# Splitting into high and low parts, moved: spread over attention slots, rounded on ScalarE in the feed-forward, half of the next norm taken forward

## The reference

```python
qkv = hidden_states @ w_qkv.T                 # 1: attention, 16 heads of 16
q, k, v = jnp.split(qkv, 3, axis=-1)
q = _rms_norm(q, q_norm_w); k = _rms_norm(k, k_norm_w)
q = _rope(q); k = _rope(k)                    # per head
scores = jnp.where(mask, q @ k^T * scale, -inf)   # causal, window of 128
out = softmax(scores) @ v
x = x + out @ w_o.T

y1 = x1 @ w_up + b_up + x1 @ w_up_lora_a @ w_up_lora_b    # 2: 256 -> 1024
x2 = relu(y1)
y2 = x2 @ w_down + b_down + x2 @ w_down_lora_a @ w_down_lora_b

proj = x @ W_xproj.T + b_xproj                # 3: selective scan
dt = softplus(dt_r @ W_dt.T + b_dt)
h = scan(exp(dt * A), dt * Bm * x);  y = sum_n h * Cm
```

## Time and profile before

| | us |
|---|---|
| median of three runs (lowest, highest) | 1144.26 (1142.16, 1153.11) |
| the profiled execution, its own time | 1144.68 |
| its span on the core | 1142.5 |

### The profile page before, as it was taken

The page is one execution under the profiler, slowest core; times in us unless marked ns, Lnnn a source line. Parts: engine busy times, 40 slices in busy tenths (PEclk is TensorE's granted clock), DMA queues, the critical chain, the costliest instruction groups (busy, mean ns, idle before and its releaser), DMA issues. The chain is left out here.

```text
span 1142.5 us, 21388 instructions
## 1 busy us (share of the span) xinstructions
PE 1038.2 (91%) x6931; PEld 908.6 (80%) x6931; DVE 800.7 (70%) x1860; ACT 689.4 (60%) x1963; POOL 650.6 (57%) x688
## 2 busy tenths in 40 slices
PE   3798987896899769999999999999979999999998
PEld 2687876685455368999999999999968888888887
DVE  6676765726888857888888888888875555555555
ACT  3455544326799758887878788877844343343432
POOL 5334312541777568786877687766634555555453
PEclk9789989898899889999999999999989999999999
DMA  9000000001224002110011000000011111111111
GB/s 254 2 1 1 2 18 5 13 1 56 95 88 144 13 1 84 47 36 3 2 47 38 1 2 2 1 2 2 1 44 30 54 41 51 45 41 55 41 46 46
DMA packets 44082, 41.58 MB, mean 36 GB/s; under 512 B 6160, under 2 KB 40048, under 8 KB 44000
## 3 DMA queue, kind: packets, MB, share of 16 engines
q1 hardware_dynamic: 42384, 39.54, 11.5%
q10 hardware_dynamic: 1616, 0.99, 0.3%
HBM read 39.40 MB, written 1.11 MB: 35 GB/s over the span
## 5 line engine op out<-in xcount | busy, mean ns | idle before, releaser
L1829 POOL TENSOR_TENSOR prob<-prob,rden 128x128 f32<-128x128 f32 (+1 forms) x256 | 127.9, 521 | 83.0 <-DVE rden L1910 81.0
L2198 POOL TENSOR_TENSOR hid_l<-hid,hid_h 128x512 fp32r<-128x512 f32 x66 | 85.4, 1294 | 133.6 <-ACT hid_h L2167 133.6
L2225 DVE TENSOR_TENSOR hid<-psum,silu 128x512 f32<-128x512 f32 x66 | 45.6, 692 | 124.7 <-ACT silu L2165 124.7
L2165 ACT ACTIVATE silu<-psum 128x512 f32<-128x512 f32 x66 | 39.5, 598 | 115.3 <-PE psum L75 115.3
L2217 DVE SCALAR_TENSOR_TENSOR x<-psum,weight,x 128x256 f32<-128x256 f32 x264 | 108.9, 476 | 0.0
L73 PE MATMUL psum<-xt_h,gu_l 128*128 128x512 f32 x264 | 106.0, 402 | 0.3 <-DVE xt_l L167 0.3
L1775 ACT ACTIVATE prob<-psum,neg_max 128x128 f32<-128x128 f32 (+1 forms) x256 | 104.9, 420 | 0.2
L75 PE MATMUL psum<-xt_h,gu_h 128*128 128x512 f32 x264 | 104.8, 397 | 0.0
L74 PE MATMUL psum<-xt_l,gu_h 128*128 128x512 f32 x264 | 104.5, 396 | 0.0
L1300 POOL TENSOR_TENSOR drive<-u,b_all 128x1024 f32<-128x1024 f32 x32 | 75.6, 2365 | 41.9 <-DVE h L1416 20.6
L1812 POOL TENSOR_TENSOR qr<-r_part_a,r_part_b 128x512 f32<-128x512 f32 x64 | 82.7, 1292 | 6.5 <-DVE r_part_b L1867 6.5
(11 more groups left out here) (281 smaller groups left out, 3748.2 us busy)
## 6 DMA issues: line engine op xcount, KB each, us to landing
b_all<-scan_b_rows SPq DMA_DIRECT2D x16, 512.0 KB, 3.9
early<-in_L_ffn_Wq_dram SPq DMA_DIRECT2D x4, 1024.0 KB, 5.8
early<-in_L_ffn_Wo_dram SPq DMA_DIRECT2D x4, 1024.0 KB, 6.0
raw<-in_L_ffn_Wg_dram SPq DMA_DIRECT2D x32, 128.0 KB, 2.2
raw<-in_L_ffn_Wu_dram SPq DMA_DIRECT2D x32, 128.0 KB, 2.3
raw<-in_L_ffn_Wd_dram SPq DMA_DIRECT2D x32, 128.0 KB, 2.3
x<-_attn_hidden_states_dram SPq DMA_DIRECT2D x8, 128.0 KB, 4.4
early<-in_L_ffn_w_up_q_dram SPq DMA_DIRECT2D x1, 1024.0 KB, 7.0
```

The lines of the kernel that those rows point to most:

```text
L1829: ins = pool.tensor_tensor(at, at, rden[:, s % 4, i:i + 1].to_broadcast([P, (i + 1) * P]), ALU.mult)
L2198: pool.tensor_tensor(hid_l[:, j, cols], hid[:, c, :], f(hid_h[:, j, cols]), ALU.subtract)\
```

## The change

1. `split` becomes two steps. `high` (ACT) stays in the slot where `split` was, for both n. `low` (DVE) stands in slots first + 1 and first + 2 for t0, in slots 9 and 10 for t1. `turn_qk` of t0: quarter 0 in first + 2, quarters 2 and 3 in first + 3, quarter 1 in first + 4, where `qk` of t1 also stands. For t1 `turn_qk` stays.
2. In the feed-forward ACT writes relu straight into `act_h` (the rounding), and then DVE computes the same relu from PSUM into `act_f` (`plain`, a tensor_scalar with add and max); POOL subtracts as before. An up bank is free when `plain` has read it. `act_h` and `act_l` have ten slots: PE makes ten up products, the four down products of half 0, six up products, the four of half 1. The down products use banks 0 and 1 alone. `norm.low` moves from after n = 4 to after n = 5; four of the eight bias additions (L1073) move behind the first down products.
3. The norm of the scan belongs to `ScanWeights`, with banks 2, 3 for half 0 and 0, 1 for half 1. Its half 0 is done inside the feed-forward: statistics after the four down products of half 0, `normalise` after n = 11, transposes on PE after n = 13, the high part on ACT ahead of n = 15, the low part after the last `plain`. The scan does half 1 alone, and PE multiplies half 0 (12 matmuls) before it transposes half 1.

```diff
@@ schedule: batches
                         if slot == first:
-                            yield "split", t0, 0
-                            yield "split", t0, 1
+                            yield "high", t0, 0
+                            yield "high", t0, 1
+                        if slot in (first + 1, first + 2):
+                            yield "low", t0, slot - first - 1
                         if slot == first + 2:
                             yield "turn_qk", t0, 0
+                        if slot == first + 3:
                             yield "turn_qk", t0, 2
-                        if slot == first + 3:
                             yield "turn_qk", t0, 3
+                        if slot == first + 4:
                             yield "turn_qk", t0, 1
-                        if slot == first + 4:
                             yield "qk", t1
                         if slot == first + 7:
-                            yield "split", t1, 0
-                            yield "split", t1, 1
+                            yield "high", t1, 0
+                            yield "high", t1, 1
+                        if slot in (9, 10):
+                            yield "low", t1, slot - 9
@@ quantized_ffn: ACT
+                    if n == 2 * KF - 1:
+                        nxt.scalar(act, (0,))
                     act.wait_ge(up_done, n + 1)
-                    if n >= 4:
-                        act.wait_ge(a_lo, n - 3)
-                    act.activation(act_f[:, n % 4, :], psum[:, UPB[n % 4], :], ACT.Relu,
-                                   bias=bias_up[:, m:m + 1]).then_inc(relu_done, 1)
+                    act.activation(act_h[:, slot(n), :], psum[:, UPB[n % 4], :], ACT.Relu,
+                                   bias=bias_up[:, m:m + 1]).then_inc(a_hi, 1)
@@ quantized_ffn: DVE
+                def plain(n):
+                    dve.wait_ge(a_hi, n + 1)
+                    if n >= 4:
+                        dve.wait_ge(a_lo, n - 3)
+                    dve.tensor_scalar(act_f[:, n % 4, :], psum[:, UPB[n % 4], :], bias_up[:, n % KF:n % KF + 1], 0.0, ALU.add,
+                                      ALU.max).then_inc(a_f, 1)
...
+                for n in range(KF + EARLY, 2 * KF):
+                    plain(n)
+                    if n == KF + EARLY + 1:
+                        nxt.normalise(dve, core.x, 0)
@@ quantized_ffn: PE
+                for n in range(KF, KF + EARLY):
+                    up(n)
+                pe.wait_ge(w_lo, 4)
+                for t in range(TH):
+                    down(t)
+                for n in range(KF + EARLY, 2 * KF):
+                    up(n)
+                    if n == 2 * KF - 3:
+                        nxt.tensor(pe, (0,))
@@ selective_scan: PE
-                for m in range(KD):
-                    for c in range(2):
-                        norm.ready(pe, c)
+                norm.ready(pe, 0)
+                for c in range(2):
+                    if c == 1:
+                        norm.tensor(pe, (1,))
+                        norm.ready(pe, 1)
+                    for m in range(KD):
```

More of the change, by code:

```diff
@@ L343, in schedule @@
             for n in range(2):
-                yield "split", 0, n
+                yield "high", 0, n
+                yield "low", 0, n
             yield "low_rest",
@@ L348, in schedule @@
             for n in range(2):
-                yield "split", 1, n
+                yield "high", 1, n
+                yield "low", 1, n
             for u in range(3):
@@ L563, in turn_o @@
                                    ACT.Copy).then_inc(o_hi, 1)
[L565 removed]
+                run(dict(qk=qk, v=copy_v, high=high, turn_qk=turn_qk, exp=exp, turn=turn, turn_o=turn_o, turn_rest=turn_rest,
                          dequantize=dequantize, next_turn=next_turn))
@@ L969, in quantized_ffn @@
     with scope:
-        norm = ffn.norm
+        norm, nxt = ffn.norm, scan.norm
+        EARLY = 2
         up_s, down_s = ffn.up_s, ffn.down_s
@@ L976, in quantized_ffn @@
         act_f = sb("act_f", [P, 4, HALF], F32)
-        act_h, act_l = (sb(f"act_{n}", [P, KF, HALF], F32R) for n in "hl")
+        act_h, act_l = (sb(f"act_{n}", [P, KF + EARLY, HALF], F32R) for n in "hl")
         shift = sb("ln1_shift", [P, TH], F32)
@@ L1373, in _ @@
             def _(dve):
-                norm.vector(dve, core.x)
                 own = norm.count
+                norm.stats(dve, core.x, 1)
+                norm.normalise(dve, core.x, 1)
+                norm.low(dve, 1)
                 def rest(k):
```

159 lines of the change are left out of this document (87 added, 72 removed).

## The result

| | before | changed |
|---|---|---|
| runs beside each other | 6 | 6 |
| median (lowest, highest), us | 1145.16 (1142.16, 1153.11) | 1133.11 (1128.07, 1135.74) |
| profiled execution, its own time | 1144.68 | 1135.74 |
| its span | 1142.5 | 1133.9 |

The medians lie 12.05 us apart (1.1%), and no run of one kernel reaches into the range of the other; the ratio taken over the rounds is 0.986 (95% interval 0.981 to 0.990), so the gain by it is a little more than the medians give. The forecast was 1134. The work is the same: the page's line of PE, the answer to the earlier trace rows (busy us, share, xinstructions), shows the same 6931 matmuls.

A forecast was written before the change was run, and what follows sets the result against it. PE, busy 91% of the span, was taken as the bound, with its pauses and the lower clock behind them. Attention -5.9, feed-forward -2.6 and start of the scan -2.2 sum to -10.7 from 1144.68: 1134 us, range 1126 to 1142.

The forecast's parts named there:

- Attention, idle: First attention, PE's waits: shorter pauses in three batches save 4.4 us, joined copies of k cost 1.5.
- The copies of k: First attention: t0's copies now stand together and delay qk of t1, 0.5 us in each of three batches, 1.5.
- Attention, clock: First attention: two slow stretches behind 2.3 us pauses cost 4.5 us; two thirds, 3.0, taken as saved (ends 0, 7.9).
- Feed-forward: Feed-forward: pause -3.1, clock -2.2, against +0.3 in an up product and +2.4 of transposes and waits: -2.6 us.
- the fourth down product: Feed-forward, second half: ends 13.8 to 15.7 us after half 0's last down product, 14.8 taken, against 15.3 before.
- the eight transposes: Feed-forward, second half: half 0's norm transposes on PE take 0.95 us, half as many at twice the clock.
- Start of the scan: Start of the scan: begins 2.9 us earlier at full clock or 1.5 at half; 2.2 taken, and it arrives whole.
- B: Attention: the wait only moves, from pt to stack; the stage gives 1.5 instead of 5.9 us, 1138.4; chance 0.13.
- C: Feed-forward: DVE and POOL alternate, normalise yields; at most 2.8 us more, another 2.2 of slow clock, 1139; chance 0.12.
- D: More gain: attention's whole 4.5 of clock, the slow stretch from 66.8 (3.4), the feed-forward's good end (1.0): 1128; chance 0.15.
- E: Attention, slower: joined copies of k make qk of t1 wait 2.3 us or more, slow clock behind: 1151.3; chance 0.05.
- F: Whole kernel: nothing of the gain comes through, 1144 us; chance 0.05.

The follow-up runs named there:

- e13_second_tile_only: Kernel before with high and low set apart for the second tile t1 of each batch alone; median 1140.48 us, ratio 0.990.
- e2_no_attention: Changed kernel with the old places of high, low and turn_qk in the first attention; median 1143.44 us, ratio 0.995.
- e12_before_again: Kernel before, unedited, profiled a second time; attention ended at 207.09 us against 196.99, and the median column gives 1159.05 in brackets.
- e3_whole_norm: Changed kernel with the scan's norm whole at the start of the scan again; median 1133.44 us, ratio 0.986.
- e5_eight_slots: Changed kernel with eight slots, no up product of half 1 before the down products of half 0; median 1136.23 us, ratio 0.986.
- e7_filled: Changed kernel with eight extra matmuls, their result overwritten, in PE's pause at the start of the scan; median 1132.55 us, ratio 0.983.
- e6_k_apart: Changed kernel with the two pairs of copies of k of t0 in separate slots; median 1130.84 us, ratio 0.981.
- e1_attention: Kernel before with only the new places of high, low and turn_qk in the first attention; median 1138.46 us, ratio 0.990.
- e10_change_again: Changed kernel, unedited, run once more in a later set beside the kernel before; median 1133.14 us, ratio 0.985.

## Why the prediction came out, step by step

**The total** was right (1134 against 1133.11), in part by luck: the steps missed in both directions, 3.0 us too little up to the first scan instruction, and 5.15 given back where I had put 0. The pair of profiles on which the sum rests lies 8.6 us apart by the spans (1142.5 and 1133.9), the medians 12.05, and my 10.7 falls between them. The mechanisms of the first three stages, though, are the ones that I had named.

**Attention, idle.** Forecast -4.4 + 1.5 = -2.9, measured -3.65. The three pauses of over 2 us before `values` went entirely: the 0.8 us that I charged for `low` beside POOL came out at 0.5 in one place, since DVE got there first. The copies of k cost 2.2 (3 x 0.7), more than the 1.5 taken, inside the ends 0 and 2.8 each.

**Attention, clock.** This is the mis-sized term: I took 3.0 of the 4.5 us behind the two pauses, since slow stretches also come without one. Measured: -5.00. e13_second_tile_only and e2_no_attention show that those two stretches hang on the pauses of t1: without them 1.00, with them 0.66 and 0.57 (means of somewhat longer stretches). Two more things made up the 5.00 that I had not seen. I wrote that there was one slow stretch besides, from 66.8, but the trace before has others: 166 to 170 (3.99 us busy at 0.57, an estimated 1.7 us), which is gone now, and one at the attention's end. That one has grown, from 2.90 us busy at 0.61 (193 to 196.99) to 3.99 at 0.55 (182 to 188.34), an estimated 0.7 us more; so -4.5 - 1.7 + 0.7 = -5.5 by estimate. And e12_before_again shows that the price of a pause is no fixed number: one execution paid 10 us more for the same pauses. I had read one execution's 4.5 us as the price. The timed runs of the kernel before spread over 21 us (1140.36 to 1161.40, 56 runs in five sets), those of the changed one over 8 (1128.07 to 1135.74, 12 runs in two), which fits this but doesn't show where it comes from.

**Feed-forward.** Forecast -2.6, measured -3.39. The new operation took 0.74 (0.7 taken) and the pause came down to 1.19 (1.5 taken). The Trainium skill ("VectorE: DVE Perf Modes", Why PSUM operands drop a tier) says that float32 out of PSUM is held to the 1x mode, which spoke against the edit. The trace agrees on the length (0.74 against 0.41), but DVE's cast alone is not the price of the old form, which was up to 1.5 us beside POOL. What the prediction calls the fourth down product is number 4 counted from 0, the first of half 1: it ended 14.1 us after the last of half 0, where I had 14.8. Of the single terms the eight transposes were too small, 0.95 against 1.41 us (the eight of half 1 at 251.70, at full clock): I had halved the time of one at the low clock, and it came down only from 0.23 to 0.18 us. The clock gave less than the 2.2: the slow stretch behind the old pause is gone, but the one from the attention's end now runs on to 197, at 0.54 from 188.34. What I did not see is that the half norm costs all of what it brings (e3_whole_norm).

**Start of the scan.** Forecast -2.2 as the mean of 2.9 and 1.5, by whether the clock holds. It did not: -1.71. The other case is seen in e5_eight_slots, -2.89 with the pause in place, and in e7_filled, -2.98 (26.70 against 29.68).

**The rivals.** B (the wait moves to `stack`) is false for the changed kernel, but e6_k_apart shows that it can: 3.3 us, against 0.5 in the changed kernel and 1.8 in e1_attention. C is true in its mechanism (2.74 us for four `normalise`, 1.4 expected alone) and false in its price, since PE waited only 0.55. D was right to want the whole 4.5, but the stretch of 66.8 that it counted too is still there (66 to 74). E, the slower side, is false: the waits on `k_t` are 0.7 us each, far under the 2 it needed. F is false.

**What stays open.** Why the 5.15 us are given back. They lie in slow stretches at four fixed places, above all in the last, whose length differs between executions of one kernel. The same code took 853.44 and 857.31 us in two executions of the kernel before, 858.59 and 856.85 in two of the changed one, and 853.54 to 859.86 in the experiments. Neither an effect of the change nor its absence can be shown from so few. The timed runs lose less than the pair of profiles does: there the two kernels lie 12.05 us apart by medians, and 1150.10 - 1133.14 = 17.0 in the set with e10_change_again, against 8.6 by the spans of the two profiles, of which the one of before is a short execution (1144.68 among the 1140.36 to 1155.55 of that set). Nor is it shown what starts the slow stretch at full load at the start of the experts (848 in the changed kernel). Whether t0's spreading is worth anything is open too: e13_second_tile_only and e1_attention end alike.

## What to carry to other kernels

An engine that works in order stands behind its longest piece of preparation: put that piece behind what the busiest engine waits for next, and split it, but then measure each piece of the split alone, since here half of it (the second tile's) brought all that the stage's end shows (187.19 against 187.41). Before taking work forward into another stage, ask what it delays there: the half norm saved 1.71 us and cost 1.83, until it stood behind the up products. And price a pause of a matrix engine by more than one execution: its idle time nearly repeats, the clock behind it does not.

## What the runs showed of the hardware

- After pauses of 2.0 to 2.3 us the granted clock fell to half, for 3.4 to 21 us, and stayed down with PE 98% busy (112 to 133 us in e12_before_again). Not always: the pause at 52.8 before is followed by 1.00 up to 66.8, the like one at 53.91 in e13_second_tile_only by 0.62 over the 9 us from 54, and the 2.31 us before 157.76 in e12_before_again by 1.00.
- A clock of 0.53 also comes over 11 us in which PE was busy all the time (848 to 859 in the changed kernel).
- With eight matmuls, 2.09 us, in a pause of 2.01 us the clock was 1.00 behind it, in two profiles of two; with the bare pause it fell in six of seven.
- A DVE tensor_scalar (add, max) of 128x512 float32 out of PSUM took 0.736 to 0.752 us in all sixteen cases, with POOL at work or not; a cast of the same size out of SBUF took 0.41 to 1.52.
- Busy time of equal code (after the first scan instruction) differed by up to 6.6 us of 812 between profiles, and between two executions of the kernel before by 10.4 of 135 in the attention, where idle time differed by 0.3.
